# Mixture-of-experts kernel on one core: list transfers placed earlier in GpSimd's order, and the third plain column's rows transposed by DMA in place of TensorE

## The reference

```python
scores = einsum('ntd,ed->nte', x, gate_w)        # x here: layernorm of the first layer's output
probs  = softmax(scores, axis=-1)                # 8 experts
g, m   = top_k(probs.transpose(0, 2, 1), 512)    # each expert picks 512 of a batch's 2048 tokens
h      = einsum('nekf,efd->nekd', gelu(einsum('nekd,edf->nekf', x[batch, m], w1)), w2)   # 512 -> 2048 -> 512
out    = zeros.at[batch, m].add(g * h)
```

## Time and profile before

| | |
|---|---|
| median of 3 runs | 1655.98 us (1655.0 to 1656.74) |
| profiled execution, its own time | 1658.91 us |
| its span | 1657.1 us |
| TensorE busy | 1641.7 us (99%) |
| VectorE, ScalarE, GpSimd busy | 1074.7, 942.8, 476.6 us |
| list transfers | 160, 171.1 us of GpSimd |

### The profile page before, as it was taken

The page is one execution under the profiler, slowest core; times in us unless marked ns, Lnnn a source line. Parts: engine busy times, 40 slices in busy tenths (PEclk is TensorE's granted clock), DMA queues, the critical chain, the costliest instruction groups (busy, mean ns, idle before and its releaser), DMA issues.

```text
span 1657.1 us, 22979 instructions
## 1 busy us (share of the span) xinstructions
PE 1641.7 (99%) x8348; PEld 1405.0 (85%) x8348; DVE 1074.7 (65%) x1938; ACT 942.8 (57%) x2045; POOL 476.6 (29%) x537
## 2 busy tenths in 40 slices
PE   9999999999999999999999999999999999999997
PEld 9999999878888878888888888888888888888886
DVE  7555697777764438655765586558655856686663
ACT  5678776735333565466546664666466646654441
POOL 3233233377477770300230033003200420040003
PEclk9999999999999999999999999999999999999999
DMA  3243436365426694412442244234323432351004
GB/s 134 77 140 115 153 119 226 127 152 127 131 54 180 128 178 151 102 29 85 136 108 53 84 119 102 76 85 101 95 77 96 96 89 77 102 97 57 26 1 51
DMA packets 140357, 171.27 MB, mean 103 GB/s; under 512 B 68141, under 2 KB 69321, under 8 KB 140249
## 3 DMA queue, kind: packets, MB, share of 16 engines
q1 hardware_dynamic: 120441, 136.04, 27.5%
q0 software_dynamic: 19776, 33.78, 11.3%
q10 hardware_dynamic: 32, 0.03, 0.0%
HBM read 121.42 MB, written 33.72 MB: 94 GB/s over the span
## 4 chain that ended last, share of the span: by engine, by line
PE 95%; ACT 1%; DMA 1%; DVE 1%; issue 0%; POOL 0%; POOLq 0%; SPq 0%; ACTq 0%; DVEq 0%
PE ps L2282 10%; PE ps L2280 10%; PE ps L2281 10%; PE ps L2260 9%; PE ps L2258 9%; PE ps L2259 9%; PE ps L1254 4%; PE ps L1255 4%; PE ps L1256 4%; PE ps L2195 3%; PE ps L2182 3%; PE ps L2184 3%; PE ps L2183 3%; PE ps L2196 3%; PE ps L2197 3%; DMA turned_planes<-planes 1%
## 5 line engine op out<-in xcount | busy, mean ns | idle before, releaser
L2280 PE MATMUL ps<-v2h,hhS 128*128 128x512 f32 x768 | 298.9, 389 | 0.0
L2282 PE MATMUL ps<-v2h,hlS 128*128 128x512 f32 x768 | 298.9, 389 | 0.0
L2281 PE MATMUL ps<-v2l,hhS 128*128 128x512 f32 x768 | 298.9, 389 | 0.0
L1646 POOL DMA_INDIRECT out_dram<-YS,tok_pair x40 | 86.4, 2161 | 682.8 <-DVE YS L2091 673.7
L2259 PE MATMUL ps<-Tl,Wh 128*128 128x512 f32 x672 | 261.5, 389 | 0.0
L2258 PE MATMUL ps<-Th,Wh 128*128 128x512 f32 x672 | 261.5, 389 | 0.0
L2260 PE MATMUL ps<-Th,Wl 128*128 128x512 f32 x672 | 261.5, 389 | 0.0
L1612 POOL DMA_INDIRECT list<-pairs,list_at x160 | 171.1, 1069 | 49.3 <-issue 48.2
L1833 ACT ACTIVATE v2h<-w_raw 128x512 fp32r<-128x512 f32 x96 | 57.5, 622 | 215.0 <-PE ps L2282 215.0
L2281 PEld LDWEIGHTS ps<-v2l,hhS 128*128 128x128 f32 x768 | 144.2, 188 | 30.0
L2282 PEld LDWEIGHTS ps<-v2h,hlS 128*128 128x128 f32 x768 | 144.2, 188 | 29.8
(11 more groups left out here) (297 smaller groups left out, 3692.9 us busy)
## 6 DMA issues: line engine op xcount, KB each, us to landing
w_raw<-in_L_ffn_w_dram SPq DMA_DIRECT2D x80, 1024.0 KB, 7.3
XB<-in_x_dram SPq DMA_DIRECT2D x16, 512.0 KB, 4.0
XR<-in_x_dram SPq DMA_DIRECT2D x16, 512.0 KB, 6.4
out_dram<-X SPq DMA_DIRECT2D x16, 512.0 KB, 5.0
xn_rows<-XN SPq DMA_DIRECT2D x16, 512.0 KB, 5.3
list<-pairs,list_at POOLq DMA_INDIRECT x160
w_raw<-in_L_xattn_Wq_dram SPq DMA_DIRECT2D x1, 1024.0 KB, 8.4
wo_sb<-in_L_xattn_Wo_dram SPq DMA_DIRECT2D x2, 512.0 KB, 11.0
```

What stands on the lines that cost most here:

```text
L2280: nc.tensor.matmul(ps[:, bank, :], th, wh, start=(t == 0), stop=False)
L2281: nc.tensor.matmul(ps[:, bank, :], th, wl, start=False, stop=False)
L2282: last = nc.tensor.matmul(ps[:, bank, :], tl, wh, start=False, stop=(t == GF - 1))
```

## The change

1. `TURNED` gets the key `(2,)`: column 2's rows are split, DMA-transposed and put together like those of columns 1 and 3. The chunks on TensorE in slots 27 to 30 (`turn`, `TURNS_1`) are gone, with their evictions. `SPLIT_AT`, `WORDS_AT` and `CHUNKS_AT` become tables by column: for i = 1 (the transposing of column 2, done in column 1's slots) both splits are in slot 13 of the column (n = 29), the words of the halves in slots 14 and 15 (n = 30, 31), all four chunks in slot 15 (n = 31). Columns 1 and 3 keep their places.
2. In SyncE's list the two DMA transposes of column 2 come after `sp_weights(9)`.
3. In GpSimd's list one list moves ahead of the gather of column 2 (two lists stand between `scatter(0)` and it, not one), all later ones move up by one, and none is left behind `scatter(2)`.

```diff
-        TURNED = ((1,), (3,), (0, 1), (0, 0)) + tuple((x, b) for x in range(1, NS) for b in range(B))
+        TURNED = ((1,), (2,), (3,), (0, 1), (0, 0)) + tuple((x, b) for x in range(1, NS) for b in range(B))
...
-        SPLIT_AT, WORDS_AT, CHUNKS_AT = (10, 11), (12, 13), {14: (0, 1), 15: (2, 3)}
+        SPLIT_AT = {i: {13: (0, 1)} if i == 1 else {10: (0,), 11: (1,)} for i in range(3)}
+        WORDS_AT = {i: {14: (0,), 15: (1,)} if i == 1 else {12: (0,), 13: (1,)} for i in range(3)}
+        CHUNKS_AT = {i: {15: (0, 1, 2, 3)} if i == 1 else {14: (0, 1), 15: (2, 3)} for i in range(3)}
...
-        TURNS_1 = tuple(range(KF // 2 + 3, KF - 1))
...
-                if gg in (G, 3 * G):
+                if gg in (G, 2 * G + 1, 3 * G):
                     for a in range(2):
-                        sp_turn(sp, (gg // G,) if gg == G else (3,), a)
+                        sp_turn(sp, (gg // G,), a)
...
             scatter(0)
-            write_lists(3, 4)
+            write_lists(3, 5)
             pool_gather(pool, 2)
-            write_lists(4, 6)
+            write_lists(5, 7)
             scatter(1)
             pool_gather(pool, 3)
             gather_pair(0, 1)
-            write_lists(6, 9)
+            write_lists(7, 10)
             gather_pair(0, 0)
             scatter(2)
-            write_lists(9, 10)
```

More of the change, by code:

```diff
@@ L1548, in xattn_expert_choice @@
         found_of = {q: m for m, q in FOUND_AT.items()}
-        def turn(n):
-            i, f = divmod(n, KF)
-            return TURNS_1.index(f) if i == 1 and f in TURNS_1 else None
         def sp_experts(sp):
@@ L1707, in act_token_chunk @@
         def act_token_chunk(act, i, k, bank):
-            act.wait_ge(f_tr, i // 2 * KD + k + 1)
+            act.wait_ge(f_tr, i * KD + k + 1)
             nc.scalar.activation(eTh[i % 2][:, k, :], ps[:, bank, :], ACT.Copy).then_inc(f_eTh, 1)
@@ L1750, in slot @@
                     act_normalise(act, X1[:, u], rs2, nb2, XN2[:, u], g_nb2, a_xn2, NBLK - 1)
-                k = turn(n - 1)
-                if k is not None:
-                    act_token_chunk(act, (n - 1) // KF + 1, k, 6)
                 i, f = divmod(n, KF)
                 if (i + 1,) in TURNED:
-                    if f == SPLIT_AT[0]:
+                    for a in SPLIT_AT[i].get(f, ()):
                         act.wait_ge(f_rows, 16 * CT * (i + 2))
[L1758 to L1762, removed]
+                        act_split((i + 1,), a)
+                    for a in WORDS_AT[i].get(f, ()):
+                        act_words(act, (i + 1,), a)
+                    for k in CHUNKS_AT[i].get(f, ()):
                         act_turned_chunk(act, i + 1, k)
@@ L1936, in slot @@
                                         ALU.subtract).then_inc(f_h, 1)
-                k = turn(n - 1)
-                if k is not None:
-                    dve_token_chunk(dve, (n - 1) // KF + 1, k, 6)
                 i, f = divmod(n, KF)
                 if (i + 1,) in TURNED:
-                    for k in CHUNKS_AT.get(f, ()):
+                    for k in CHUNKS_AT[i].get(f, ()):
                         dve_turned_chunk(dve, i + 1, k)
@@ L2216, in slot @@
                     pe_round(pe, 1, rounds_in(n)[0])
-                if turn(n) is not None:
-                    pe_token_chunk(pe, n // KF + 1, turn(n), 6)
                 if n % KF == KF - 1:
```

## The result

The changed kernel takes 1666.99 us (median of 4 runs, 1665.52 to 1671.55), the kernel before 1656.36 us on the same chip (4 runs, 1655.0 to 1658.2). The ratio is 1.0068 with a 95% interval of 1.0045 to 1.0091. The forecast was 1654.4 us, "no change that can be told", with a range up to 1659.5: the time lies 7.5 us outside it, on the slow side.

A forecast was written before the change was run, and what follows sets the result against it. TensorE, busy 99% of the span, was taken to set the time. Column 2 cost +1.5 us, pair (0, 1) resumed as before and saved 1.6 us of slow clock: -1.6 us in all, 1655.98 to 1654.4 us, range 1650.0 to 1659.5.

The forecast's parts named there:

- The chunks that go: TensorE in column 1's slots: dropping four transpose chunks of 0.52 us each saves 2.1 us.
- rival 1: Waits at column 2 and pair (0, 1) both go: gain 2.1 + 3.8 = 5.9 us, 1650.1 us; chance 0.17.
- When the first half of column 2 lands: Column 2's first DMA transpose lands at 481.2, the middle of 479.6 and 482.7; bounds 476.3 and 484.5.
- The due time: End of column 1: `down(31)` is due at 484.6, so a landing after 479.2 stalls TensorE by the excess.
- The slow clock: After column 2's 2.0 us stall TensorE runs at the lower clock, charged 1.6 us, 3.6 us with the stall.
- the first part of the change: Column 2 in sum: -2.1 for chunks, +3.6 for stall and clock, +1.5 us, between -2.1 and +5.8.
- GpSimd's queue: The moved list makes column 2's gather and everything up to column 2's scatter come 4.5 us later.
- Pair (0, 1): Second half still lands at 605.2, TensorE waits 0.7 us and resumes at 611.4, winning the slow clock's 1.6 us.
- I let the two cancel: At pair (0, 1), help from removed list transfers equals harm from the scatter 4.5 us later; landing stays at 605.2.
- rival 4: Scatter 4.5 us later delays pair (0, 1)'s second half to 605.2 + 4.5: +4.5 us, 1660.5 us; chance 0.20.

The follow-up runs named there:

- e9: Changed kernel, column 2's transposes issued ahead of the weight loads, scatter of column 2 and list reads held until pair (0, 0)'s transposes landed: 1653.02 us, 0.9964.
- e11: Changed kernel, old list order, column 2's splits in slots 11 and 12, transposes ahead of weight loads, scatter and list 9 held past pair (0, 0)'s transposes: 0.9962.
- e12: Changed kernel, with GpSimd's lists 5 and 6 held until column 2's transposes have landed: ratio 1.0053.
- e8: Changed kernel, with SyncE issuing column 2's two transposes ahead of the weight loads: 1653.93 us, 0.9977.
- e4: Kernel before, with list 9 held until pair (0, 0)'s transposes have landed, the scatter of column 2 left in place: ratio 0.9981.
- e6: Changed kernel, with the scatter of column 2 and the list reads behind it held until pair (0, 0)'s transposes have landed: 1659.92 us, 1.0019.
- e10: Changed kernel, with column 2's transposes ahead of the weight loads and GpSimd's list order as before the change: ratio 1.0008.
- e3: Kernel before, with the scatter of column 2 held until pair (0, 0)'s transposes have landed, list 9 following the last gather at once: ratio 0.9987.
- e2: Changed kernel (column 2's rows by DMA), with GpSimd's list order as before the change: 1659.81 us, 1.0015.
- e7: Changed kernel, with only the ten list reads held until pair (0, 0)'s transposes have landed, the scatter left in place: ratio 1.0032.

## Why the prediction was wrong, step by step

**The chunks that go.** Right: 16 matmuls fewer, 2.1 us forecast and 1.9 read; with both places cured (e9, e11) the gain fits the 2.1 + 3.8 us that the forecast's rival 1 had as the most.

**When the first half of column 2 lands.** This is the first step that failed. The forecast took the middle of 479.6 and 482.7, "481.2", with 484.5 as the bound; it was 484.3. The steps behind it held: 5.35 us from the landing to `down(31)` gives 489.65, and it started at 489.96. The due time (484.6) held within 0.3 as well, since 489.96 - 5.05 = 484.9. What was off is the landing, by 3.1 us, because the row used was column 3's 9.3 us, where the loads were issued 8.9 us ahead. The forecast did correct for the shorter lead, but averaged the corrected number with the uncorrected one; the corrected 482.7 was the nearer. e12 and e8 show that loads close in front and lists beside cost far more together at this place than either without the other, and no row of before had them so close together.

**The slow clock.** The forecast charged the one price seen, 1.6 us. A longer wait cost more: 2.6 us after 5.05 us, 2.8 after 7.17. So the price at column 2 was 5.2 + 2.6 = 7.8 us in place of 3.6, and the first part of the change +5.9 in place of +1.5 (the bound was +5.8).

**GpSimd's queue.** The forecast moved it by 4.5 us. The gather of column 2 started 11.3 us later (453.09, before 441.75), the last gather 11.7 (588.76, before 577.04). The list that was moved was priced at 20.7 us, like list 3; the two lists took 453.09 - 406.01 = 47.1, since single issues were longer (3.02 us for the one at 435.67, usually 0.96), and they began 1.7 us later than list 3 did before (404.36). Why issues stretch is open. Landing weights do not explain the longest, since the DMA engines were nearly still around it (us, busy by engine, granted clock, DMA share, GB/s):

```profile
435.00:436.00 1.00, 1.00 (x6) 0.81 (x5) 1.00 (x2) 0.00 (x0) 0.69 (x2) 1.00 0.23 17
436.00:437.00 1.00, 1.00 (x6) 0.84 (x5) 1.00 (x1) 0.41 (x1) 1.00 (x1) 1.00 0.01 1
437.00:438.00 1.00, 1.00 (x7) 0.81 (x6) 1.00 (x2) 0.23 (x1) 1.00 (x1) 1.00 0.00 0
```

**Pair (0, 1).** "I let the two cancel" is the step that did most of the damage: the forecast had -3.1 us there (from +1.5 to -1.6) and 5.2 + 1.2 = +6.4 were measured, 9.5 us off, where column 2 was 4.4 off. The list taken away is worth 4 us there (e4), but the scatter did not move 4.5 us onto the transposes: by queue it moved 11.8 (594.05, before 582.20), and the transposes moved 5.9. Relative to them it came 5.9 us later, from 2.3 us ahead of the first issue to 3.6 behind it, and all of it was issued by 600.7, ahead of both landings (605.4 and 616.4). That is rival 4, given 0.20, with its mechanism as written: a landing 605.2 + 4.5 was its price, 616.4 was measured. e6 shows that with the scatter held nothing is left of it, and e9 that the gather alone, which moved along with it (from 7.5 us ahead of the first issue to 1.7), does not make it. A part of the 5.2 us may be the gather's.

**The place where the two parts meet** was not in the forecast at all. It added the lateness of column 2 and the change at the pair as separate terms, and even counted a delay at column 2 as partly hidden by the wait behind it. In fact the landing is no fixed time: the issue moves with TensorE, and so does what lies beside it. Without the delay at column 2 the new list order keeps the scatter behind the transposes (e8, 0.9977); with the old order it does not (e10, 1.0008). Of the two edits neither is bad by itself in every company; the order of two DMAs in SyncE's list decides.

## What to carry to other kernels

One and the same DMA transpose took from 4.8 to 14.9 us from issue to reader in these runs, by what lay beside it and in front of it: before moving a DMA, list what is in front of it in its queue and what other queues issue beside it in the next 15 us, and take the price from a row with the same company, or else only a bound. Even then it is a range: the same place with the same company gave up to 3 us more or less. Where two stages share such a transfer, a delay in the first moves the second's transfer onto other traffic, so the terms don't add. And when an average of two estimates is formed from one corrected for the difference at hand and one that is not, the corrected one is the estimate.

## What was not expected of the hardware

- A DMA transpose of 512 KB inside SBUF was seen at its reader 4.8 to 6.2 us after issue with either lists or loads as its company at column 2, but 9.9 with lists alone at the pair in e12; 8.2 just behind a gather with lists beside (e3), 10.9 beside gather and scatter (e4), 12.6 to 14.7 with 2 MB of loads just in front and lists beside (e2, e6, the change, e7), although the lists move only 16 KB for each 16 transfers.
- An indirect DMA of a list took GpSimd 0.96 us to issue as a rule and once 3.02 us, with the DMA engines nearly still; 32 of them took 47.1 us where twice list 3 of the kernel before is 41.4 (2 x 20.7).
- The slow clock took more after a longer wait: 12 matmuls cost 5.28 us after 5.05 us of idle time, and 24 cost 8.27 after 7.17, against 2.7 and 5.44.
